# Two 64-wide attention layers: products that shared one PSUM bank and one pair of semaphores get banks and semaphores of their own

## What is computed

```
# "rows" layer (L1) and "keys" layer (L3); 16 heads of width 64, inner width 1024
xn = layernorm(x)                                  # per token, eps 1e-5
q, k, v = xn @ Wq, ctx @ Wk, ctx @ Wv              # each (8, 256, 1024)
s = per head (q @ k.T) * 64 ** -0.5  (+ mask)      # 256 x 256 per head
x = x + concat_heads(softmax(s) @ v) @ Wout (+ bout)
```

## Time and profile before

| what | value |
|---|---|
| runs shown | 1849.26, 1849.54, 1855.38 us; median 1849.54 |
| the profiled execution | 1852.31 us, its span 1850.5 us |
| mean granted TensorE clock in it | 0.924 of full speed |
| busy share of the span | PE 82%, DVE 59%, ACT 48%, POOL 39% |
| instructions | 28608 |

### The profile page before, as it was taken

How to read it: one execution, slowest core, us unless ns; L and a number is a source line. 1 busy time by engine, 2 the same in 40 slices (tenths; PEclk the granted TensorE clock), 3 DMA queues, 4 the chain that set the end, 5 groups by cost and what they waited for, 6 DMA issues and landing times.

```text
span 1850.5 us, 28608 instructions
## 1 busy us (share of the span) xinstructions
PE 1516.0 (82%) x9445; PEld 964.8 (52%) x9457; DVE 1083.9 (59%) x2348; ACT 894.8 (48%) x1947; POOL 712.7 (39%) x1039
## 2 busy tenths in 40 slices
PE   5787789999998575766766888699889999997798
PEld 2443346666565465666663444444456656665343
DVE  4453456676765666777674544433376666665444
ACT  1434346666665366665551444243266665563222
POOL 4442134444443576777763332100044444433000
PEclk8999789999999689888888999799899999997899
DMA  1006000000000000000000000000000000000000
GB/s 59 15 13 253 0 4 4 6 3 3 3 3 1 1 1 1 1 0 0 1 0 10 7 7 4 23 1 0 3 4 4 3 3 3 3 0 1 1 11 11
DMA packets 13668, 21.72 MB, mean 12 GB/s; under 512 B 3200, under 2 KB 10256, under 8 KB 13072
## 3 DMA queue, kind: packets, MB, share of 16 engines
q1 hardware_dynamic: 13584, 20.63, 3.2%
HBM read 19.58 MB, written 1.05 MB: 11 GB/s over the span
## 4 chain that ended last, share of the span: by engine, by line
PE 52%; DVE 23%; ACT 13%; issue 7%; POOL 4%; DVEq 0%; ACTq 0%; DMA 0%; SPq 0%; POOLq 0%
ACT sb_both L966 8%; DVE sb_VP L664 5%; PE bank L1565 5%; DVE bank L1043 4%; PE bank L906 4%; PE bank L888 4%; PE bank L863 3%; PE bank L399 3%; DVE sb_wneg L1045 3%; POOL sb_QT L748 3%; PE bank L1776 3%; PE bank L1956 3%; DVE sb_both L1735 3%; PE bank L852 2%; PE bank L1784 2%
## 5 line engine op out<-in xcount | busy, mean ns | idle before, releaser
L1111 POOL TENSOR_TENSOR sb_both<-sb_both,sb_winv 128x512 f32<-128x512 f32 x256 | 260.8, 1039 | 410.2 <-DVE sb_winv L1050 410.2
L1663 POOL TENSOR_TENSOR sb_KM<-sb_OT 128x1024 f32<-128x1024 f32 x128 | 247.2, 1969 | 91.4 <-DVE sb_both L1735 87.3
L966 ACT ACTIVATE sb_both<-bank,sb_wneg 128x256 f32<-128x256 f32 x512 | 235.5, 476 | 27.6 <-DVE sb_wneg L1045 26.4
L1565 PE MATMUL bank<-sb_ident,sb_both 128*128 128x128 f32 x1024 | 162.3, 326 | 103.9 <-DVE sb_both L1735 70.4
L1735 DVE SCALAR_TENSOR_TENSOR sb_both<-sb_KM,sb_best,bank 128x1024 f32<-128x1024 f32 x128 | 159.7, 1272 | 93.6 <-ACT bank L1637 93.2
L1565 PEld LDWEIGHTS bank<-sb_ident,sb_both 128*128 128x128 f32 x1024 | 149.2, 172 | 120.3 <-DVE sb_both L1735 76.2
L664 DVE TENSOR_REDUCE sb_VP<-bank 128x8 f32<-128x2048 f32 (+1 forms) x64 | 111.1, 1757 | 93.6 <-PE bank L405 93.6
L1045 DVE TENSOR_REDUCE sb_wneg<-bank 128x4 f32<-128x1024 f32 x128 | 156.8, 1225 | 4.4
L1637 ACT ACTIVATE bank<-sb_KM 128x1024 f32<-128x1024 f32 x128 | 130.3, 1026 | 49.0 <-DVE sb_both L1735 34.6
L906 PE MATMUL bank<-sb_QT,sb_VP 128*64 128x256 f32 x1024 | 142.4, 400 | 13.3 <-DVE sb_QT L1057 13.3
L875 PE MATMUL bank<-sb_KM 64*128 64x256 f32 x1024 | 147.1, 406 | 2.5 <-ACT sb_both L966 2.5
(11 more groups left out here) (257 smaller groups left out, 2733.6 us busy)
## 6 DMA issues: line engine op xcount, KB each, us to landing
sb_ctxT_in<-in_ctxT SPq DMA_DIRECT2D x32, 128.0 KB, 2.3
sb_F<-in_F SPq DMA_DIRECT2D x2, 1024.0 KB
sb_XO<-in_ctx SPq DMA_DIRECT2D x8, 128.0 KB, 2.1
sb_WQ<-in_WQ SPq DMA_DIRECT2D x2, 512.0 KB, 5.8
sb_WK<-in_WK SPq DMA_DIRECT2D x2, 512.0 KB, 6.9
sb_WV<-in_WV SPq DMA_DIRECT2D x2, 512.0 KB, 7.7
sb_WO<-in_WO SPq DMA_DIRECT2D x2, 512.0 KB, 8.6
sb_WKQ<-in_WKQ SPq DMA_DIRECT2D x1, 1024.0 KB, 9.2
```

The lines of the kernel that those rows point to most:

```text
L966: last = act.activation(PRW[:, t % 4, h, i, :], s[:, h, i, :], ACT.Exp, bias=wneg[:, t % 4, h, i:i + 1], accum_out=wsum[:, t % 4, h, i:i + 1])
L1111: pool.tensor_tensor(p, p, winv[:, t % 4, :, i:i + 1].broadcast_to([P, 2, SEQ]), ALU.mult).then_inc(w_norm, 1)
L1565: last = pe.matmul(weight_bank(c), gated[:, h % 4, c * P:(c + 1) * P], ident[:], is_transpose=True, start=(h == 0 and c % 4 == 0), stop=(h ...
L1663: pool.tensor_tensor(dst, s[:, h, 0, :].unsqueeze(2).broadcast_to([P, NK, NK]), s[:, h, 1, :].unsqueeze(1).broadcast_to([P, NK, NK]), ALU. ...
```

## The change

The one list of uses and the pair `w_fill`, `w_drain` go. Four kinds of product get a semaphore pair each: queries and keys (`w_qk`, `w_qk_out`), values (`w_v`, `w_v_out`), turned norm (`w_ln`, `w_ln_out`), output product (`w_out`, `w_added`). Queries and keys stay in bank 7. Values and turned norm move to bank 6, beside the weighted products; the output product moves to bank 5, beside the transposes. Waits that keep the shared banks 5 and 6 apart are new. In step 3 the output product now comes ahead of the queries and keys. Before the first step, the value product v0 now comes ahead of the queries and keys of pair 1. The arithmetic, its shapes, its counts and the engines that do it are unchanged.

```diff
 # TensorE
-            def put(part, b, use):
+            def norm(b):
+                pe.wait_ge(xn_ready, A.xn + TPB * b + TPB)
+                if not known_below(b, 1):
+                    pe.wait_ge(w_ot, A.pairs + PAIRS * b - 5)
+                for i in range(TPB):
+                    last = pe.transpose(bank[6][:, i * P:(i + 1) * P], xn[:, i, :], ident[:])
+                last.then_inc(w_ln, 1)
+            def queries_keys(b, j):
+                g = pair(b, j)
+                if not known_below(g, 1):
+                    pe.wait_ge(w_qk_out, g)
+                if j == 0:
+                    pe.wait_ge(ctx_ready, A.ctx + b + 1)
+                    pe.wait_ge(w_ln_out, A.batches + b + 1)
+                pe.matmul(bank[7][:, 0:SEQ], WQ[:, j * P:(j + 1) * P], xnT[:], start=True, stop=True)
+                pe.matmul(bank[7][:, SEQ:2 * SEQ], WK[:, j * P:(j + 1) * P], ctxT[:],
+                          start=True, stop=True).then_inc(w_qk, 1)
+            def values(b, u, weighted_so_far):
+                half_, kt = u // 2, u % 2
+                if weighted_so_far is not None:
+                    pe.wait_ge(w_ot, A.pairs + weighted_so_far)
+                elif u == 0:
+                    pe.wait_ge(w_ln_out, A.batches + b + 1)
+                else:
+                    pe.wait_ge(w_v_out, A.values + 4 * b + u)
+                pe.matmul(bank[6][:], ctxT[:, kt * P:(kt + 1) * P], WV[:, half_ * GROUP:(half_ + 1) * GROUP],
+                          start=True, stop=True).then_inc(w_v, 1)
+            def out_product(b, turned):
+                pe.wait_ge(w_ot, A.pairs + PAIRS * (b + 1))
+                pe.wait_ge(w_pt[1], A.pairs + turned)
+                for i in range(TPB):
+                    for j in range(PAIRS):
+                        last = pe.matmul(bank[5][:, i * D:(i + 1) * D], OT[:, j, i * P:(i + 1) * P], WO[:, j, :],
+                                         start=(j == 0), stop=(j == PAIRS - 1))
+                last.then_inc(w_out, 1)
 # in transposes, second half, into bank 5
+                    if t == 1 and i == 1 and not known_below(b, 1):
+                        pe.wait_ge(w_added, A.batches + b)
 # in weighted, into bank 6
-                if t % 4 == 0:
-                    half_ = t // 4
-                    part = "first" if isinstance(b, int) and b == 0 else "last" if isinstance(b, int) else "loop"
-                    pe.wait_ge(w_drain, A.before_use(part, b, "v3" if half_ else "v1") + 1)
+                if t in (0, 4):
+                    pe.wait_ge(w_v_out, A.values + 4 * b + (2 if t == 0 else 4))
+                elif t in (1, 2):
+                    pe.wait_ge(w_v_out, A.values + 4 * b + t + 2)
+                elif t in (3, 5, 6) and not (isinstance(b, int) and b == BATCH - 1):
+                    if t == 3:
+                        pe.wait_ge(w_ln_out, A.batches + b + 2)
+                    else:
+                        pe.wait_ge(w_v_out, A.values + 4 * b + t)
 # step
                 scores(b, t)
+                if t == 3 and behind:
+                    out_product(b - 1, PAIRS * b + 1)
                 if t < 6:
-                    put(part, b, f"qk{t + 2}")
+                    queries_keys(b, t + 2)
                 elif more:
-                    put(part, b, f"qk{t - 6}")
-                if t == 3 and behind:
-                    put(part, b, "out")
+                    queries_keys(b + 1, t - 6)
...
+                weighted_so_far = PAIRS * b + t - 2 if behind or t >= 3 else None
 # before the first step
-            for use in A.USES["pre"]:
-                put("pre", 0, use)
+            norm(0)
+            queries_keys(0, 0)
+            values(0, 0, None)
+            queries_keys(0, 1)
 # VectorE (ScalarE's copy of queries and keys changes in its semaphores alone)
+            def norm_out(b):
+                dve.wait_ge(w_ln, A.batches + b + 1)
+                if not known_below(b, 1):
+                    dve.wait_ge(w_qk, A.pairs + PAIRS * b)
+                dve.tensor_copy(xnT[:], bank[6][:, 0:SEQ]).then_inc(w_ln_out, 1)
+            def values(b, u):
+                half_, kt = u // 2, u % 2
+                dve.wait_ge(w_v, A.values + 4 * b + u + 1)
+                if not known_below(b, 1):
+                    dve.wait_ge(w_av, A.pairs + PAIRS * (b - 1) + (4 if half_ == 0 else PAIRS))
+                dve.tensor_copy(VW[:, kt, half_ * GROUP:(half_ + 1) * GROUP], bank[6][:]).then_inc(w_v_out, 1)
+            def add_out(b):
+                dve.wait_ge(w_out, A.batches + b + 1)
+                if A.kind == "rows":
+                    dve.wait_ge(biased, b + 1)
+                xb = x[:, bass.ds(TPB * b, TPB), :]
+                dve.tensor_tensor(xb, bank[5][:, 0:SEQ].rearrange("p (i d) -> p i d", i=TPB), xb, ALU.add)\
+                   .then_inc(w_added, 1)
```

More of the change, by code:

```diff
@@ L53 @@
 class Wide:
-    USES = {"pre": ("ln", "qk0", "qk1", "v0"),
[3 rows of a table removed]
-            "epi": ("out",)}
-    TIMES = {"pre": 1, "first": 1, "loop": BATCH - 2, "last": 1, "epi": 1}
     def __init__(self, kind, base, number):
@@ L66, in __init__ @@
         self.pairs = number * BATCH * PAIRS
[L67 to L71, removed]
+        self.batches, self.values = number * BATCH, number * BATCH * 4
         self.after = dict(base, ctx=base["ctx"] + BATCH, xn=base["xn"] + TPB * BATCH, ln=base["ln"] + BATCH,
                           stat=base["stat"] + 7 * BATCH, stages=base["stages"] + 1)
-    def before_use(self, part, b, use):
-        n = self.use0[part] + self.USES[part].index(use)
-        return n + (b - 1) * len(self.USES["loop"]) if part == "loop" else n
 class Narrow:
@@ L837, in pair @@
                 return A.pairs + PAIRS * b + t
-            def put(part, b, use):
[L840 to L858, removed]
-                else:
[L860 to L865, removed]
@@ L922, in step @@
                     transposes(*back_by(b, t, 2))
+                weighted_so_far = PAIRS * b + t - 2 if behind or t >= 3 else None
                 if t == 0:
-                    put(part, b, "v1")
+                    values(b, 1, weighted_so_far)
                 if t in (3, 4):
-                    put(part, b, f"v{t - 1}")
+                    values(b, t - 1, weighted_so_far)
                 if t == 5 and more:
-                    put(part, b, "ln")
+                    norm(b + 1)
                 if t == 7 and more:
-                    put(part, b, "v0")
+                    values(b + 1, 0, weighted_so_far)
             pe.wait_ge(stage_done, A.stages)
@@ L943, in wide_tensor, with queries_keys @@
             weighted(last_b, 7)
-            put("epi", BATCH, "out")
+            out_product(last_b, PAIRS * BATCH)
         def wide_scalar(act, A):
-            def take(part, b, use):
-                if not use.startswith("qk"):
-                    return
-                act.wait_ge(w_fill, A.before_use(part, b, use) + 1)
-                j = int(use[2:])
+            def queries_keys(b, j):
+                act.wait_ge(w_qk, pair(b, j) + 1)
                 act.activation(QK[:, j, :, :], bank[7][:].rearrange("p (a n) -> p a n", a=2), ACT.Copy)\
-                   .then_inc(w_drain, 1)
+                   .then_inc(w_qk_out, 1)
             def pair(b, t):
@@ L980, in heads_out @@
                 if t == 0 and not known_below(b, 1):
-                    part = "last" if isinstance(b, int) else "loop"
-                    act.wait_ge(w_fill, A.before_use(part, b, "out") + 1)
+                    act.wait_ge(w_out, A.batches + b)
                 act.activation(OT[:, t, :], bank[6][:, 0:SEQ], ACT.Copy).then_inc(w_ot, 1)
@@ L987, in step @@
                 if t < 6:
-                    take(part, b, f"qk{t + 2}")
+                    queries_keys(b, t + 2)
                 elif more:
-                    take(part, b, f"qk{t - 6}")
+                    queries_keys(b + 1, t - 6)
                 if behind or t >= 3:
@@ L997, in wide_scalar @@
             act.wait_ge(stage_done, A.stages)
-            for use in A.USES["pre"]:
-                take("pre", 0, use)
+            queries_keys(0, 0)
+            queries_keys(0, 1)
             wide_parts(act, step)
@@ L1069, in step @@
                 if t == 3 and behind:
-                    take(part, b, "out")
+                    add_out(b - 1)
                 if behind or t >= 2:
@@ L1073, in step @@
                 if t == 0:
-                    take(part, b, "v1")
+                    values(b, 1)
                 if t in (3, 4):
-                    take(part, b, f"v{t - 1}")
+                    values(b, t - 1)
                 if t == 5 and more:
-                    take(part, b, "ln")
+                    norm_out(b + 1)
                     take_context(dve, A, b + 1)
                 if t == 7 and more:
-                    take(part, b, "v0")
+                    values(b + 1, 0)
             normalise(0)
@@ L1091, in wide_vector @@
```

(8 more changed lines are left out.)

18 lines of the change are left out of this document (2 added, 16 removed), and 3 rows, old and new, of the table USES.

## The result

The changed kernel takes **1802.7 us** (median of 4 runs, 1800.85 to 1804.69) against 1849.88 before: ratio 0.9733, 95% interval 0.9717 to 0.9748, 47 us less. The forecast was 1811.5 in a range of 1800 to 1829: the sign, the place and the mechanism came out, the gain was 9 us larger than the 38 forecast. Runs of the kernel before spread more than the 0.3% named at the top: seven beside one of the later experiments lie between 1842.54 and 1863.44.

What follows compares the result with a forecast made beforehand. TensorE was taken as the bound. Waits gone, 50.9 us, less 13.3 given back made 37.6; counting batches made 40; 38 off the 1849.54 median gave 1811.5 us, own range 1804 to 1819, with two rivals 1800 to 1829.

Steps and rivals of the forecast that it cites:

- TensorE sets the pace, not the loop: In the layers: TensorE's work, 40.71 us a batch, leads VectorE's and ScalarE's reciprocal-to-exponentials cycle, eight steps of 4.59, 36.7 us.
- The values' copy is allowed 1.06 us more; 0.66 stays: Bank 6, weighted product: later need covers stalls of 0.19 and 0.53; of 1.19, 0.66 us stays in 12 batches.
- The output product's 1.46 goes whole: Step 3: in bank 5, ahead of the projection, the output product no longer waits 1.46 us for ScalarE's projection copy.
- A loop batch of 41.44 us: Batch in mid-layer: 40.71 of work plus 0.66 stall plus 0.07 for the norm, 2.64 less than 44.08.
- The start: I take 2.4 off: Layer starts: of 4.3 us of waits in both layers, 2.4 counted as hidden under the first exponentials, so not gained.
- the sum by batches: Second count of the gain: five loop batches, a last one and the first with the start, 20.0 us a layer, 40 in all.
- Registers, 1.2 us, and the bound of 12: Added waits: one more on VectorE in step 0 costs 1.2 us; TensorE's cost nothing, at most 12 us.
- The first (waits reappear whole): Value waits return whole at the weighted product, or new waits cost their bound: 1824 to 1828 us, chance 0.14.
- The second, nothing left: No stall remains as VectorE's steps close up: 40.7 us a batch, 11 us more gained, 1800 us, chance 0.09.
- The third, the falling clock: Steady batches, bank 6 hand-offs: TensorE's clock falls; slower from 5.8% at low level, 1877 us at 10%, chance 0.03.
- The fourth: Bank 6, five times a batch: values and norm wait for ScalarE's copy; 1868 us at 0.7 each, chance 0.03.
- between them 38: The gain forecast for the whole kernel: 38 us, taken between 37.6 by waits and 40 by batches.

Runs made afterwards that it cites:

- the last experiment: In the changed kernel, VectorE's statistics for the next batch moved behind the value copy in step 0: 1799.1 us, then 1795.9 beside the changed kernel's 1802.6.
- the experiment's expectation: Against the changed kernel, ScalarE's heads' copy put behind its copy of the turned probabilities, expected near 1890 us: measured 1886.3 us, ratio to before 1.0172.
- the last two experiments: Both against the changed kernel: ScalarE's heads' copy put behind the turned probabilities' copy, 1886.3 us; VectorE's statistics put behind the value copy, 1799.1 and 1795.9 us.
- the run with the old start: The changed kernel with the first value product back behind the queries and keys of pair 1: 1812.5 us, ratio to before 0.9813.
- the filled drain: The kernel before with four unused products into bank 7 in each layer's drain: 1851.3 us against 1853.9, ratio 0.9984.

## Why the prediction was right, and where its sizes were off

**TensorE sets the pace, not the loop.** Right. Undoing one part returned its waits in the bodies: 23.1 us for 19.5 us of the output product's waits, 18.7 for 24.3 of the values' less the 5.8 at the weighted product. Nothing hid them. In reading the prediction gives ScalarE 27.9 and GpSimd 19.2 us; the row has 27.55 and 20.10. Both are far under TensorE's 41.9, so nothing hangs on it.

**The values' copy is allowed 1.06 us more; 0.66 stays.** Right: 0.56 measured, 13 waits instead of 12 (the thirteenth in the first batch). Its cause, the statistics ahead of the copy, was shown by moving them: the 0.56 went, and with it 6.3 us of the bodies; the total fell by 3.8 and by 6.7.

**The output product's 1.46 goes whole.** Right, and by the bank, not by the order. The walk's 0.9 us of cover at the transposes held. Taking the bank back cost 1.65 us a batch: the 1.46, and 0.19 more, as projection and output product in a row without a wait take 4.64 us where the walk had 4.83.

**A loop batch of 41.44 us.** Measured 41.19 and 41.18: 0.10 less stall, those 0.19, and 0.04 more before the first projection. That is 0.25 over five batches of the first layer. In the second layer a batch took 43.9 before, so it won 2.72 where 2.64 stood. Together 1.7 us of the missing 9.

**"The start: I take 2.4 off".** This is the term that was mis-sized. Of 4.3 us of waits it kept 1.9 for both layers (the sum by batches, 1.2 a layer, had 2.4); the starts gained 4.8. The two waits ahead of the first scores, 0.75 and 0.69 us in each layer, went whole, 2.9 in all: the "0.5 more a layer" were not hidden, since these two waits come before the first exponentials. The rest, 1.9, is put down to the clock by argument: without those waits it rose ahead of the first scores in five of the changed kernel's six starts. Behind the first scores, the first batch and the step to the next gained 4.6 in the first layer where 3.6 stood (the body's 21.3 less 5 x 2.89 and 2.2 for the last batch), and 5.0 in the second. The first scores at the higher level are 0.94 of that in each layer; the sum had no term for this. So 2.4 us of the 9 are the starts, against the sum by batches, and 2.4 the first batches.

**Registers, 1.2 us, and the bound of 12.** TensorE's added waits are free, as taken. For VectorE's one more wait no cost showed up in the stall either. The last 2 us of the 9 lie in "between them 38": the sum by batches was 40. All these terms missed to the same side.

**The rivals.** The first (waits reappear whole) falls with 5.8 us of waits. The second, nothing left, was wrong by the 0.56, and is what the last experiment makes of it: 40.64 a batch, the 40.7 that it named. The third, the falling clock, was wrong in its place: the steady batches stay at 1.00 at 44.48 of 45 us busy. The Trainium skill, TensorE: Matmul & The Clock Gate, in its section on a second HAM failure mode, tells of a bf16 kernel that cycled through PSUM banks and whose clock went back and forth at the micro-idles between its groups of products; the trace of these float32 batches does not show that, before or after the change. The clock does move at the layers' ends, where TensorE waits 2.45 us at a time, and in the stages between. The fourth did not come, and was right as a price: at five places a batch the experiment's expectation made it 88 us, and 84 were measured. No wait for the heads' copy shows in the changed kernel, whose ScalarE copies the heads first.

The Trainium skill, Perfetto Trace Analysis, under Optimizing Tensor Performance, advises that independent groups of products rotate through PSUM banks so that one's evacuation overlaps the next one's products. The trace agrees, with a condition that the last two experiments put in numbers: it helps as far as the evacuation's place in the other engine's order keeps up, by 0.43 us here with ScalarE, and short by 0.56 with VectorE.

**Signs that were named.** Output products 41.2 us apart (41.4 named), no wait for the projection's copy before them, TensorE busy 44.48 of 45 us, 98.8%. The reciprocals of steps 6 and 7 are 4.60 and 4.59 us behind the ones before (400.83, 405.43, 410.02), within the 4.6.

**Open:** the total of the run with the old start (10 us for 3 to 4 us of start; its drains ran at a lower clock), and whether the filled drain lowers the clock of later stages or only happened to meet it.

## What to carry to other kernels

Before a shared buffer is split, walk one period with the other engines' own order: what a split wins is the room between the old user and the new one (1.06 us here), what it risks is each new hand-off's cover (0.43 us here, worth 84 us when lost). In a period that one engine fills, as TensorE does here, a wait taken away pays one for one, and the next lever is the small work that stands ahead of the copy which that engine waits for. Differences in stages that the change doesn't touch, and in drains full of idle time, go by the clock: cut the spans into parts and repeat the profile before giving them to the change.

## What was not expected of the hardware

A drain with idle times of 1.6 and 2.5 us ran at a granted clock of 1.00 in some executions of one kernel and fell to the lower level in others: 18.5 us or 23.5 for the same instructions. The stages between the layers, the same in all these kernels, took 718 to 729 us at a granted clock of 0.89 to 0.86. And 384 more semaphore waits in TensorE's stream, all already met and most against register values, did not lengthen the spacing of its output products (41.18 us against 41.19).
